# A block of an early-fusion transformer: the down projection of the experts, by rows in float32 or by columns in split fp32r

## The reference

```python
h = h + attention(layernorm(h))     # 12 heads of 16, q and k normed (RMS) and rotated, causal
x = layernorm(h)
shared = (silu(x @ sg) * (x @ su)) @ sd                 # 192 -> 384 -> 192
probs = sigmoid(x @ router_w + routing_bias)            # three experts
scores, indices = top_k(probs, 2); scores /= scores.sum(-1, keepdims=True)
combine_w = (one_hot(indices, 3) * scores[..., None]).sum(-2)
out_e = (silu(x @ gate_e) * (x @ up_e)) @ down_e        # each expert, 192 -> 384 -> 192
h = h + shared + sum over e of out_e * combine_w[e]
```

## Time and profile before

| | us |
|---|---|
| median of 3 runs | 1615.61 |
| lowest, highest | 1614.32, 1616.34 |
| profiled execution | 1612.98 |
| its span in the trace | 1611.2 |
| TensorE busy in it | 1573.3 |
| VectorE busy | 1184.5 |
| ScalarE busy | 879.8 |
| GpSimd busy | 408.7 |

### The profile page before, as it was taken

How to read it: one execution, slowest core, us unless ns; L and a number is a source line. 1 busy time by engine, 2 the same in 40 slices (tenths; PEclk the granted TensorE clock), 3 DMA queues, 4 the chain that set the end, 5 groups by cost and what they waited for, 6 DMA issues and landing times.

```text
span 1611.2 us, 46325 instructions
## 1 busy us (share of the span) xinstructions
PE 1573.3 (98%) x16536; PEld 1471.8 (91%) x16536; DVE 1184.5 (74%) x3383; ACT 879.8 (55%) x1896; POOL 408.7 (25%) x647
## 2 busy tenths in 40 slices
PE   6899999999999999999999999999999999999999
PEld 6699999999999999999999999999999999998988
DVE  6776777767777777777677777677777677877665
ACT  4555554556545565545566555566555566555552
POOL 0332321232311323212323212323212323212320
PEclk8999999999999999999999999999999999999999
DMA  6211221111211112211111111111111111110110
GB/s 219 76 38 58 69 69 38 49 58 62 69 49 45 53 59 69 68 34 47 45 49 57 52 39 37 49 49 57 49 42 40 47 49 57 51 41 32 36 33 13
DMA packets 75381, 86.80 MB, mean 54 GB/s; under 512 B 12720, under 2 KB 64328, under 8 KB 75208
## 3 DMA queue, kind: packets, MB, share of 16 engines
q1 hardware_dynamic: 64776, 65.45, 11.9%
q10 hardware_dynamic: 10560, 20.74, 4.0%
HBM read 32.44 MB, written 12.51 MB: 28 GB/s over the span
## 4 chain that ended last, share of the span: by engine, by line
PE 87%; DMA 5%; DVE 5%; SPq 1%; issue 1%; ACT 1%; POOL 0%; DVEq 0%
PE ps L426 79%; PE ps L429 6%; DMA kt<-kt 5%; DVE kt L1174 1%; DVE o L1071 1%; PE ps L626 1%; DVE rotated L1162 1%; SPq L368 1%; DVE xt L1102 1%; DVE qk_split L1167 1%; DMA router_bias<-in_b_router 0%; ACT wf L809 0%; DVE stats L1091 0%; POOL rstd L1014 0%; ACT xt L809 0%
## 5 line engine op out<-in xcount | busy, mean ns | idle before, releaser
L426 PE MATMUL ps<-xt,wf 64*128 64x326 f32 x6912 | 592.7, 316 | 0.0
L426 PEld LDWEIGHTS ps<-xt,wf 64*128 64x128 f32 x6912 | 522.6, 186 | 11.4 <-issue 5.6
L426 PE MATMUL ps<-w_down_s,ht 128*128 128x192 f32 (+1 forms) x2304 | 414.0, 329 | 0.0
L426 PEld LDWEIGHTS ps<-w_down_s,ht 128*128 128x128 f32 (+1 forms) x2304 | 350.9, 174 | 14.4 <-issue 0.2
L1048 DVE SCALAR_TENSOR_TENSOR gated<-tanh_g,ps 128x326 f32<-128x326 f32 x384 | 189.0, 492 | 199.0 <-ACT tanh_g L823 199.0
L816 ACT ACTIVATE rows<-h,rstd 128x192 f32<-128x192 f32 (+2 forms) x279 | 151.1, 564 | 211.2 <-POOL rstd L1018 206.4
L1007 POOL TENSOR_TENSOR probs<-probs,causal 128x512 f32<-128x512 f32 x192 | 228.7, 1191 | 132.0 <-ACT probs L834 132.0
L834 ACT ACTIVATE probs<-ps 128x792 f32<-128x792 f32 (+1 forms) x384 | 254.4, 663 | 13.3 <-PE ps L426 12.8
L823 ACT ACTIVATE tanh_g<-ps 128x326 f32<-128x326 f32 x384 | 169.9, 442 | 164.6 <-PE ps L426 163.0
L1001 POOL TENSOR_TENSOR probs<-probs,causal 69x140 f32<-69x140 f32 x192 | 88.9, 463 | 474.0 <-ACT probs L834 473.9
L1054 DVE TENSOR_TENSOR ht<-gated,ps 128x326 f32<-128x326 f32 x384 | 190.1, 495 | 13.1
(11 more groups left out here) (105 smaller groups left out, 1957.4 us busy)
## 6 DMA issues: line engine op xcount, KB each, us to landing
kt<-kt SPq DMA_DIRECT2D x384, 40.8 KB, 1.8
x_s<-in_xp ACTq DMA_DIRECT2D x40, 384.0 KB, 3.1
qt<-qt SPq DMA_DIRECT2D x132, 81.5 KB, 1.9
residual<-h SPq DMA_DIRECT2D x31, 288.0 KB, 2.4
out<-o SPq DMA_DIRECT2D x32, 192.0 KB
qt<-qt ACTq DMA_DIRECT2D x60, 81.5 KB, 2.0
kept_rows<-embed_rows SPq DMA_DIRECT2D x44, 96.0 KB, 1.7
h<-kept_rows SPq DMA_DIRECT2D x30, 95.2 KB
```

What stands on the lines that cost most here:

```text
L426: return nc.tensor.matmul(dst, lhs, rhs, start=first, stop=last)
```

## The change

The down projection is turned round. The weights (128 of their 192 columns in `w_down_hi` and `w_down_lo`, the other 64, high and low side by side, in `w_down_rest`) are stationary, and 326 columns of activations move, so the result lies by columns and all four experts are added up in two PSUM banks. Weights and activations are split in high and low parts of fp32r: ScalarE rounds each activation to `h_high` (`round_h`), and the rest `h_low` is subtracted by VectorE for the shared expert and by GpSimd for the routed ones (`low_h`). In the last turn, without attention, VectorE subtracts all. Three products give the first 128 columns (`down_main`) and two the others (`down_rest`), for each of twelve units.

Since experts are summed in PSUM, the routing weights go onto the activations first. The exponentials are turned behind the first unit, the picks follow among the units, TensorE turns the nine rows of weights ahead of the sixth unit (`weights_turn`), VectorE copies them to `weight_held` (`hold_weights`, between the sixth `gate` and `up`), SP stores them in DRAM and loads them again, spread over all partitions (`spread_weights`), and GpSimd multiplies them onto the nine routed activations behind the masks (`weigh`). ScalarE copies the sum to `out_cols`, TensorE turns it to rows (`out_turn`), and at the beginning of the next turn VectorE adds it in four operations to `o` (`sum_out`), onto which a DMA has copied `h1`.

The moments of the first norm are taken a unit later, and its inverse root one pair of masks later. `h_high` and `qk_split` now lie in the memory of `probs`, and `h_low` in that of `ht`. In the opening ScalarE and VectorE split the down weights (two operations each of 1536 and 768 columns) where VectorE halved them. The core of the diff:

```diff
-SUMS = 2 * FFNS
+SUMS = 2
+ROUTED = UNITS - CHUNKS
+EARLY_HIGH = 7
+WEIGHTS_UNIT = 5
...
-        ht = sb("ht", [P, UNITS, COLS])
+        ht, h_low = under("ht", [P, UNITS, COLS], ("h_low", [P, UNITS, COLS], F32R))
+        weight_cols = sb("weight_cols", [P, EXPERTS, COLS])
+        weight_held = sb("weight_held", [EXPERTS * TILES, P])
+        out_cols = sb("out_cols", [P, 2, COLS])
...
+            def store_out(b):
+
+                sp.wait_ge(summed.sem, summed.at(b, SUMS))
+                sp.dma_start(out[b, 0:2 * P, :].rearrange("(t p) d -> p t d", p=P), o[:, 0:2, :]).then_inc(stored.sem, 16)
+                sp.dma_start(out[b, 2 * P:TOKENS, :], o[0:REAL2, 2, :]).then_inc(stored.sem, 16)
+                sp.wait_ge(stored.sem, stored.at(b, 32))
+
+            def spread_weights(b):
+
+                sp.wait_ge(weights_held.sem, weights_held.at(b, 1))
+                sp.dma_start(weight_rows, weight_held[:]).then_inc(weights_stored.sem, 16)
+                if later(b):
+                    sp.wait_ge(h_weighted.sem, h_weighted.at(b - 1, ROUTED))
+                sp.wait_ge(weights_stored.sem, weights_stored.at(b, 16))
+                sp.dma_start(weight_cols[:], weight_spread).then_inc(weights_loaded.sem, 16)
...
             def turn(i, at, N, D, T, L, A, F):
                 b0, b1, b2, b3 = i + 2, i + 1, i, i - 1
+                sp.wait_ge(h1_ready.sem, h1_ready.at(b3, 1))
+                if later(b3):
+                    store_out(b3 - 1)
+                sp.dma_start(o[:], h1[:]).then_inc(o_copied.sem, 16)
+                spread_weights(b3)
...
                 for t in range(TILES):
-                    last = turned(ps[:, ROUTE_BANK, t * P:(t + 1) * P], route_e[:, t * P:(t + 1) * P], P)
+                    last = mm(ps[:, ROUTE_BANK, t * P:t * P + R_COLS], route_e[0:H, t * P:(t + 1) * P], ident[0:H, 0:R_COLS],
+                              True, True)
                 last.then_inc(route_turned.sem, 1)
...
-                for c in range(CHUNKS):
-                    last = mm(accumulator(e, t, L, A), ht[:, CHUNKS * e + c, tile_cols(t)], w_down_s[:, CHUNKS * e + c, :],
-                              c == 0, c == CHUNKS - 1)
...
+            def weights_turn(b):
+
+                pe.wait_ge(pick_chain.sem, pick_chain.at(b, 7))
+                pe.wait_ge(h_ready.sem, h_ready.at(b, WEIGHTS_UNIT - 2))
+                turned(weights_at, route[:, 6].rearrange("p t e -> p (t e)"), P).then_inc(weights_turned.sem, 1)
...
+            def down_main(units, b, A):
+
+                for k in units:
+                    if k == 0 and not later(b):
+                        pe.wait_ge(s_down_low, 2)
+                    wait_low(k, b, A)
+                    acc = ps[:, DOWN_BANK, 0:COLS]
+                    mm(acc, w_down_hi[:, k, :], h_low[:, k, :], k == 0, False)
+                    mm(acc, w_down_lo[:, k, :], h_high[:, k, :], False, False)
+                    last = mm(acc, w_down_hi[:, k, :], h_high[:, k, :], False, k == UNITS - 1)
+                    if k == UNITS - 1:
+                        last.then_inc(down_done.sem, 1)
+
+            def down_rest(units, b, A):
+
+                for k in units:
+                    wait_low(k, b, A)
+                    w = w_down_rest[:, k].rearrange("p s c -> p (s c)")
+                    mm(ps[:, DOWN_BANK + 1, 0:COLS], w, h_low[:, k, :], k == 0, False)
+                    last = mm(ps[:, DOWN_BANK + 1, 0:COLS], w, h_high[:, k, :], False, k == UNITS - 1)
...
+            def out_turn(b):
+
+                pe.wait_ge(out_kept.sem, out_kept.at(b, 1))
+                for t in range(TILES):
+                    for a in range(2):
+                        at = (2 * (t % 2) + a) * P
+                        last = turned(ps[0:TILE_COLS[t], DOWN_BANK + t // 2, at:at + P], out_cols[:, a, tile_cols(t)], P)
+                last.then_inc(out_turned.sem, 1)
...
                 for k in range(UNITS):
-                    if F:
-                        unit(k, b3, at, D, A)
+                    if k == WEIGHTS_UNIT:
+                        weights_turn(b3)
+                    unit(k, b3, at, D, A)
+                    if k == 0:
+                        route_turn(b3, A)
                     if A:
                         score(k, b2, F)
                 if A:
                     for g in range(GROUPS):
                         value(g, b2, F)
+                if L:
+                    norm1_turn(b1, F)
                 if A:
-                    route_turn(b3)
-                    if L:
-                        norm1_turn(b1, F)
-                    down(0, 0, b3)
                     y_to_rows(b2)
-                    down(0, 1, b3)
-                    pe.wait_ge(route_seen.sem, route_seen.at(b3, 1))
-                    down(0, 2, b3)
...
+                down_main(range(0, 1), b3, A)
                 if L:
                     for t in range(TILES):
                         project_qkv(t, b1, A)
+                    pe.wait_ge(v_kept.sem, v_kept.at(b1, 1))
                 if A:
                     y_to_cols(b2, F)
...
+                down_main(range(1, 5), b3, A)
                 if A and L:
                     pe.wait_ge(v_kept.sem, v_kept.at(b1, 2))
                 if A:
                     project_y(b2)
...
+                if N:
+                    pe.wait_ge(v_kept.sem, v_kept.at(b1, 3))
+                    embed(at, N)
+                down_main(range(5, 9), b3, A)
+                down_rest(range(0, 6), b3, A)
                 if A:
                     norm2_turn(b2)
+                down_main(range(9, UNITS), b3, A)
+                down_rest(range(6, UNITS), b3, A)
                 if L:
-                    pe.wait_ge(summed.sem, summed.at(b3, 5))
-                    down(3, 0, b3)
-                    down(3, 1, b3)
                     first_groups(b1)
-                    pe.wait_ge(summed.sem, summed.at(b3, 6))
-                    down(3, 2, b3)
                     for n in range(2, 2 * GROUPS):
                         qk_turn(n, b1, at, N)
...
+                out_turn(b3)
                 if A:
                     router(b2)
...
+                    keep_y(0, b2)
+                    keep_y(1, b2)
+                    round_h(range(0, CHUNKS), b3)
+                    keep_y(2, b2)
                 if L:
                     for h in range(2):
                         keep_high(h, xt[:, 2 * h, :], XT_BANK + h, n1_turned, b1, xt_hi)
+                round_h(range(CHUNKS if A else 0, EARLY_HIGH), b3)
...
+                round_h(range(EARLY_HIGH, UNITS), b3)
...
+                act.wait_ge(down_done.sem, down_done.at(b3, 2))
+                copy(out_cols[:], ps[:, DOWN_BANK:DOWN_BANK + 2, 0:COLS]).then_inc(out_kept.sem, 1)
...
+                    nc.gpsimd.tensor_tensor(ht[:, k, :], ht[:, k, :], weight_cols[:, k // CHUNKS - 1, :],
+                                            ALU.mult).then_inc(h_weighted.sem, 1)
...
+                nc.gpsimd.tensor_tensor(h_low[:, k, :], ht[:, k, :], f32(h_high[:, k, :]), ALU.subtract).then_inc(routed_low.sem, 1)
...
-                    if L and p == 1:
+                    if L and p == 2:
                         inverse_root(i + 1, n1_moments, mean_var, rstd, n1_root, n1_ready)
+                for units in (range(CHUNKS, EARLY_HIGH), range(EARLY_HIGH, UNITS)):
+                    weigh(units, i - 1)
+                    if A:
+                        for k in units:
+                            low_h(k, i - 1)
                 if A:
                     inverse_root(i, n2_moments, mean_var2, rstd2, n2_root, n2_ready)
```

More of the change, by code:

```diff
@@ L100, in sb, with under @@
             return ctx.enter_context(nc.sbuf_tensor(name, shape, dt))
+        def under(name, shape, *others):
+            with nc.sbuf_tensor(name, shape, F32) as first:
+                pass
+            return first, *(sb(other, like, dt) for other, like, dt in others)
         def signal(name, per_batch):
@@ L699, in turn @@
                         project_qkv(t, b1, A)
+                    pe.wait_ge(v_kept.sem, v_kept.at(b1, 1))
                 if A:
                     y_to_cols(b2, F)
-                if F and L:
-                    pe.wait_ge(v_kept.sem, v_kept.at(b1, 1))
-                if F:
-                    for t in range(TILES if N == 2 else 2):
-                        down(1, t, b3)
+                down_main(range(1, 5), b3, A)
                 if A and L:
@@ L879, in turn @@
                              qkv_part(t, DIM, HALF_V).rearrange("p a (h d) -> p a h d", d=HEAD_DIM)).then_inc(v_kept.sem, 1)
+                if A and not L:
+                    for h in range(2):
+                        keep_high(h, xt[:, 2 * h, :], YT_BANK + h, yt_turned, b2, yt_hi)
+                round_h(range(EARLY_HIGH, UNITS), b3)
                 if A:
-                    if not L:
-                        for h in range(2):
-                            keep_high(h, xt[:, 2 * h, :], YT_BANK + h, yt_turned, b2, yt_hi)
```

(25 more changed lines are left out.)

217 lines of the change are left out of this document (118 added, 99 removed).

## The result

The changed kernel takes 1714.96 us (median of 4 runs, 1714.43 to 1715.49) against 1614.96 (4 runs of the kernel before, beside them). The ratio is 1.0622, 95% interval 1.0609 to 1.0635. I had forecast 1725, in a range of 1605 to 1775. The profiled execution has a span of 1712.7 us at a mean granted clock of 0.991.

The account below looks back on a forecast made before the run. TensorE, busy 98% of the span, was taken as the bound. Its saving of 1.7 us a turn plus new waits gave +3.4 a turn, +112 in all with the ends: 1725 us, range 1605 to 1775.

Parts of the forecast that it names:

- TensorE's own work: TensorE's down products, transposes and turns: less work removed than added back, saving 1.7 us a turn if nothing new waits.
- Point 1: First norm's inverse root behind the third masks delays an exponential, so TensorE waits at a score: +0.9 us a turn.
- Point 2: ScalarE's rounding of three activations before the third y copy makes TensorE wait before y's transposes: +0.5 us.
- Point 3: GpSimd's 18 operations behind the masks, 0.83 us each, ending near V+15.5 (V: end of the value products).
- Point 4: Port lock: VectorE operations with two SBUF operands slow beside GpSimd; QKV +1.4, project-y +1.9, second norm +0.4 us.
- The +0.4 at the second norm: TensorE's average wait for the second norm's scaled rows: 0.7 us in one-tile turns, nothing in double turns.
- The sum: All terms together: +3.4 us a full turn, +102 over 30 turns, +112 with the last turns and opening.
- Faster: From V to project-y: operands are ready in time, TensorE keeps its 1.7 us a turn, about 1570 us; 18%.
- GpSimd the bound: GpSimd's operations take 1.1 us, delaying the second norm's root: some 3.5 us more a turn, 1830 us; 6%.

Follow-up runs that it names:

- bare: The changed kernel, first norm's root ahead of the third masks, without roundings, rests or weighing around the down projection (parts of the result left out): 1583.5 us.
- unread: root_early with GpSimd's 18 operations replaced by products on constants into a spare buffer, TensorE taking rounded activations for routed rests: 1677.1 us.
- old_with_reads: The kernel before the change, plus 18 idle GpSimd products on constants behind the masks in each turn: 1644.7 us.
- no_gpsimd: root_early without GpSimd's nine products and nine subtractions, TensorE reading rounded activations for routed rests: 1590.5 us.
- root_early: The changed kernel with only the first norm's inverse root moved back behind the second pair of masks: 1690.8 us.
- unread_writes: unread with each of GpSimd's 18 products replaced by a product of three columns and a fill of 800 columns: 1727.8 us.
- old_with_writes: The kernel before the change, plus 14 GpSimd fills of 1024 columns a turn, each behind a product of three columns: 1619.6 us.
- xt_first: The changed kernel with VectorE's second and third shared subtractions moved behind the low halves of xt and the division of y's rows: 1757.5 us.
- reordered: root_early with fewer roundings before the third y copy, qt's first group copied earlier, and shared subtractions and down products moved: 1808.9 us.
- balanced: reordered with ten rest products ahead of project-y, the router before the output's turn, and two shared subtractions behind the second norm's moments: 1671.9 us.
- psum_rotary: balanced with VectorE's rotary products in full turns reading the QKV projection in PSUM instead of ScalarE's SBUF copy: 1636.3 us.

## Why the prediction was right, by its steps

- **TensorE's own work, -1.7 a turn.** Right. In `bare` the 30 turns from the first to the last routing exponential (127.9 to 1547.9) are 35.5 us shorter than before (124.1 to 1579.6), 1.2 a turn, with 0.46 of qt wait inside: 1.6. The down products lie 0.15 us apart (849.36, 849.51), the figure taken by columns.
- **Point 1, +0.9.** 0.59 shows as a wait before the ninth score; undoing it gave 24.2 us, 0.8 a turn. Place, cause and size right.
- **Point 2, +0.5.** Mis-sized. The transposes of y start 0.80 behind V, where the norm's six take 0.57 without a wait, and 0.62 in `bare`, which has no roundings. So the point is worth some 0.2.
- **Point 3, GpSimd.** Its operations take 0.92, not 0.83; 18 end at V+14.6, ahead of my V+15.5, since VectorE holds it up less. The root waits for the moments, not for GpSimd, as said. The Trainium skill ("GPSIMD Engine Reference", 3.1) gave an estimate of 0.9, and the changed kernel's trace has that number. It is no test of the estimate, since these operations run beside VectorE's: on constants in `unread` one takes 0.79, in `old_with_reads` 0.77.
- **Point 4, the lock, +3.7.** Right in kind, a quarter too large: `unread` less `no_gpsimd` is 86.6 us, 2.9 a turn. The step mis-sized is the extra for one operation, 0.66 from the small root steps of the opening. In a turn a sine product gains 0.25, a cosine product 0.46, a subtraction 0.48 (0.976 against 0.496). So project-y starts at V+11.49, not V+12.35, and its wait is 1.32 for 1.9; QKV waits 1.10 for 1.4. The +0.4 at the second norm does not show as a wait. Two sums of this point do not come out of their own terms: six products at 1.0 from V+5.95 end at V+11.95, not V+11.4, and V+20.6 against V+19.5 is 1.1, not 0.7. Both slips made the forecast lower.
- **Left out.** qt: ScalarE's copy to out_cols stands ahead of it, and TensorE waits 13.9 us at its transposes, 0.5 a turn.
- **The sum.** +3.4 a turn forecast; the same stretch is 89.9 us longer (128.8 to 1674.2), 3.0 a turn. The rest of the span grew by 11.6, forecast 10. Points 1, 2 and 4 were too high by 0.1, 0.3 and 0.8, against 0.5 forgotten for qt and 13.7 us (0.5 a turn) between `unread` and `root_early`. That leaves 0.2 a turn unexplained. The waits and their cause were right, but that the sum came within 10 us is partly luck, since what was too high and what was forgotten nearly cancel.
- **Rivals.** *Faster* holds in `no_gpsimd`, with no such work on GpSimd. *GpSimd the bound* came true in `unread_writes` at 0.98 us an operation.
- **Not tried:** weights multiplied by another engine with all else kept, and a clock test with filler alone.

## What to carry to other kernels

Work moved to an idle GpSimd was not free here, since it read SBUF beside a chain of VectorE's operations with two operands in SBUF. List what VectorE does in those microseconds, operation by operation, with where its operands lie; with one operand in PSUM the rotary products were not slowed. And when removing one of two waits, ask whether they have one cause: then they only merge, and in these kernels the longer wait was often followed by half the clock.

## What the runs showed of the hardware

- GpSimd's fills leave VectorE's two-operand products alone (358 ns), but a single-input one, the root's first step (TENSOR_SCALAR over 72 columns), went from 198 to 457 ns beside them, and to 524 beside the reads (the kernel before, `old_with_writes` and `old_with_reads`). I had no term for it.
- One TensorE wait of 2.1 to 2.6 us among dense products was, in most turns of `xt_first` and `reordered`, followed by a stretch of 3.4 us or more at 1.2 GHz. From the changed kernel to `xt_first` the waits for xt rise from 75.8 to 82.6 us, and the time by 42.5; by the mean clocks (0.991 and 0.960, twice the missing part of the span) 110 us more were spent at half speed.
- Both sides pay: from `balanced` to `psum_rotary`, where VectorE's rotary products no longer have two operands in SBUF, GpSimd's product goes from 0.895 to 0.838 us. In the changed kernel it is 0.92.
